# Jobs of the first layer moved in a hand-written timetable, and the second layer's first norm moved ahead of the layer boundary

## The reference, cut to what matters

```
mod = (silu(c) @ wmod).reshape(4, 6, 1, 128)            # sa, ca, ga, sb, cb, gb; |ga|, |gb| at least 0.25
# layer one
h = layernorm(x) * (1 + ca) + sa
x = x + ga * attn0(h)      # per token a 16-head recurrence: conv + silu on q, k, v, then
                           #   S = a*S - a*b*(S k) k^T + b*v k^T ;  o = q S      over 512 tokens; then @ Wo
h = layernorm(x) * (1 + cb) + sb
x = x + gb * ffn0(h)       # softmax routing, top 2 of 8 experts of 256 hidden columns
# layer two
h = layernorm(x) * (1 + ca) + sa
x = x + ga * attn1(h)      # differential causal attention, 16 heads, two softmaxes a head
h = layernorm(x) * (1 + cb) + sb
x = x + gb * ffn1(h)       # top 2 of 16 experts, plus a shared expert
```

## Time and profile before

| what | us |
|---|---|
| timed runs, in order | 1352.18, 1363.12, 1362.86 |
| median | 1362.86 |
| profiled execution | 1351.91 |
| its span, first instruction to last | 1349.8 |
| TensorE busy | 974.7 (72%) |
| VectorE busy | 836.9 (62%) |
| ScalarE busy | 583.0 (43%) |
| GpSimd busy | 442.2 (33%) |
| mean granted TensorE clock | 0.847 |

### The profile page before, as it was taken

How to read it: one execution, slowest core, us unless ns; L and a number is a source line. 1 busy time by engine, 2 the same in 40 slices (tenths; PEclk the granted TensorE clock), 3 DMA queues, 4 the chain that set the end, 5 groups by cost and what they waited for, 6 DMA issues and landing times.

```text
span 1349.8 us, 17349 instructions
## 1 busy us (share of the span) xinstructions
PE 974.7 (72%) x5737; PEld 579.8 (43%) x5737; DVE 836.9 (62%) x1960; ACT 583.0 (43%) x1409; POOL 442.2 (33%) x636
## 2 busy tenths in 40 slices
PE   5461465984986996787778788887777786865682
PEld 3231132453453553333335433454555553544482
DVE  1388879769988331766676666665656585624453
ACT  3344252462442343255454545334555543563262
POOL 0201341723733123022442244324312247323323
PEclk9785595996987997699788978669999987998797
DMA  8300000000000001000000000021244113341372
GB/s 233 94 0 0 1 0 1 1 3 33 1 1 1 1 0 40 0 1 1 1 1 1 1 1 1 1 72 59 83 126 115 61 49 119 94 117 53 116 224 83
DMA packets 54840, 60.39 MB, mean 45 GB/s; under 512 B 6224, under 2 KB 41184, under 8 KB 54752
## 3 DMA queue, kind: packets, MB, share of 16 engines
q1 hardware_dynamic: 52704, 55.10, 13.4%
q0 software_dynamic: 2048, 4.20, 1.0%
HBM read 46.05 MB, written 13.24 MB: 44 GB/s over the span
## 4 chain that ended last, share of the span: by engine, by line
PE 47%; DVE 20%; ACT 12%; issue 11%; POOL 7%; DMA 2%; SPq 0%; another core or an unknown queue 0%; ACTq 0%; DVEq 0%; POOLq 0%
PE banks L753 7%; PE banks L810 5%; PE banks L896 4%; PE banks L800 4%; PE banks L596 3%; POOL oms L1872 3%; DVE MX L1389 3%; PE banks L763 3%; PE banks L766 2%; PE banks L648 2%; PE banks L828 2%; PE banks L870 2%; ACT PT L1691 2%; PE banks L835 2%; ACT yh L1626 2%
## 5 line engine op out<-in xcount | busy, mean ns | idle before, releaser
L1389 DVE TENSOR_REDUCE MX<-banks 128x4 f32<-128x512 f32 (+2 forms) x192 | 199.2, 1043 | 89.9 <-PE banks L870 81.9
L1849 POOL TENSOR_SCALAR_AFFINE_SELECT PT<-PT 128x256 f32<-128x256 f32 x256 | 106.2, 428 | 412.2 <-ACT PT L1691 412.1
L1691 ACT ACTIVATE PT<-banks 128x768 f32<-128x768 f32 (+1 forms) x192 | 167.9, 878 | 108.4 <-PE banks L828 105.4
L753 PE MATMUL banks<-xgT,wg 128*128 128x128 f32 x616 | 89.2, 291 | 42.1 <-ACT ysb L1652 37.6
L835 PE MATMUL banks<-KS,QS 32*128 32x512 f32 (+3 forms) x512 | 97.7, 426 | 21.6 <-DVE MX L1389 17.3
L896 PE MATMUL banks<-PT,VA 128*17 128x512 f32 (+3 forms) x1024 | 98.5, 483 | 16.6 <-DVE on L1412 10.6
L800 PE MATMUL banks<-w,hid 128*128 128x128 f32 x512 | 77.1, 298 | 45.6 <-DVE hid L1334 43.4
L828 PE MATMUL banks<-QS,KS 32*128 32x128 f32 (+3 forms) x512 | 94.1, 411 | 13.9 <-ACT PT L1691 9.0
L800 PEld LDWEIGHTS banks<-w,hid 128*128 128x128 f32 x512 | 69.7, 206 | 78.9 <-DVE hid L1334 60.5
L753 PEld LDWEIGHTS banks<-xgT,wg 128*128 128x128 f32 x616 | 77.9, 199 | 55.1 <-issue 51.8
L1338 DVE SCALAR_TENSOR_TENSOR sil<-sil,yh 128x256 f32<-128x256 f32 x109 | 47.7, 438 | 61.2 <-ACT sil L1632 60.9
(11 more groups left out here) (266 smaller groups left out, 2098.1 us busy)
## 6 DMA issues: line engine op xcount, KB each, us to landing
wg<-in_ffn_dram SPq DMA_DIRECT2D x77, 386.0 KB
xg<-xs SPq DMA_DIRECT2D x17, 256.0 KB
yb<-ysb SPq DMA_DIRECT2D x17, 256.0 KB, 3.7
w<-in_ffn_w_dram SPq DMA_DIRECT2D x12, 256.0 KB
xs<-zt SPq DMA_DIRECT2D x2, 1472.0 KB, 14.2
xs<-zt SPq DMA_DIRECT2D x1, 1984.0 KB, 13.0
x<-in_L_attn_x_dram SPq DMA_DIRECT2D x4, 256.0 KB, 5.7
out_dram<-x SPq DMA_DIRECT2D x16, 64.0 KB
```

The lines of the kernel that those rows point to most:

```text
L753: mm = e.matmul(ps[:, at:at + cols], w, h, start=True, stop=True)
L1389: v_mx.at(e.tensor_reduce(MX[n % 2][:, u:u + nm, qb % 2, 2 * pair:2 * pair + 2, 24].rearrange("p s i -> p i s"), p4, AX.X, ALU.max, negate ...
L1691: a_p.at(e.activation(PT[q % 3][:, 2 * pair:2 * pair + 2, :], where["score", q, pair][:, :, 0:n], ACT.Exp, scale=ISQ8))
L1849: ins = e.affine_select(out=pt, in_=pt, compare_op=ALU.is_ge, fill=0.0, base=0, pattern=[[0, 2], [1, 128]], channel_multiplier=-1)
```

## The change

Only the tables change, and with them the order of jobs in layer one; one wait (`g_fin`) is split by tile. No operation is added or taken away.

- Post-scan jobs of groups 0 to 2: most stand 1 to 6 units of the table earlier, those of group 3 up to 3, in the part from `o_turn` to `route`.
- Experts: group 0 starts at 55 instead of 62 behind its scan with the same step of 4.6; group 1 at 55 with 3.7 instead of 4.6; group 2 at 55 with 3.1 instead of 4.0; group 3 at 39 instead of 42 with 2.7.
- Layer two's first `stat` and `norm` (batch 0) get the names `stat_x` and `norm_x` and stand at the end of layer one's table on VectorE and GpSimd: the statistics behind the last unit, the power between GpSimd's second and third `moe_x`. TensorE and ScalarE keep their part (`turn_x`) at the head of layer two.
- `stat` of layer two's batch m waits for 13 + m of the `moe_x` tiles instead of all 16.

```diff
@@ front_table
         if part == 0:
-            table += [(t - 14, ("stat", 0, 4 + b, (1, b))), (t - 9, ("norm", 0, 4 + b, (1, b)))]
+            if b:
+                table.append((t - 14, ("stat", 0, 4 + b, (1, b))))
+            table.append((t - 9, ("norm" if b else "turn_x", 0, 4 + b, (1, b))))
@@ LATE0
-    POOL=dict(stat=1.0, down=2.5, moe_x=1.0))
+    POOL=dict(stat=1.0, stat_x=2.0, down=2.5, moe_x=1.0))
@@ post_table
-        gq, state, pw, dk, ol, sums, out, step = 0, (1, 15), 5, 20, 21, (6, 20, 31), 34, 2.4
+        gq, state, pw, dk, ol, sums, out, step = 0, (1, 14), 5, 18, 19, (6, 19, 29), 31, 2.2
...
-    table += [(sums[2], ("o_sum", g, 2)), (out, ("o_tok", g)), (out + 3, ("o_turn", g)), (out + 5, ("o_out", g))]
-    table += [(out + 7 + i, ("o_x", g, i)) for i in range(3)]
-    table += [(out + 11, ("stat", 1, g, (0, g))), (out + 14, ("norm", 1, g, (0, g)))]
-    table += [(out + 19 + 1.6 * i, ("route", g, i)) for i in range(6)]
+    table += [(sums[2], ("o_sum", g, 2)), (out, ("o_tok", g)), (out + 2.5, ("o_turn", g)), (out + 4, ("o_out", g))]
+    table += [(out + 6 + i, ("o_x", g, i)) for i in range(3)]
+    table += [(out + 10.5, ("stat", 1, g, (0, g))), (out + 13, ("norm", 1, g, (0, g)))]
+    table += [(out + 17 + 1.4 * i, ("route", g, i)) for i in range(6)]
@@ table_layer0
-        table += post_table(g, SCAN[g + 1]) + moe0_table(g, SCAN[g + 1] + (62 if g < 3 else 42), (4.6, 4.6, 4.0, 2.7)[g])
-    return table
+        table += post_table(g, SCAN[g + 1]) + moe0_table(g, SCAN[g + 1] + (55 if g < 3 else 39), (4.6, 3.7, 3.1, 2.7)[g])
+    end = max(t for t, job in table if job[0] == "moe_x") - 3
+    return table + [(end + 0.5, ("stat_x", 0, 4, (1, 0))), (end + 2, ("norm_x", 0, 4, (1, 0)))]
@@ VectorE, stat
                 elif k == 0:
-                    v.wait_ge(g_fin, 16)
+                    v.wait_ge(g_fin, 13 + m)
```

More of the change, by code:

```diff
@@ L86 @@
 LATE = dict(
-    PE=dict(norm=2.0, top_t=4.0, o_back=2.5),
+    PE=dict(norm=2.0, turn_x=2.0, top_t=4.0, o_back=2.5),
     DVE=dict(top=2.0, top_t=6.0, qk_in=2.0, up=4.0, down=1.0, route=2.0, place=0.0, w_o=2.0, rms=2.5),
-    ACT=dict(score=1.0, qk_in=1.0, v_in=1.0, norm=3.0, turn=1.0, up=1.5, rms_t=1.0, route=4.0, gate_t=1.0),
+    ACT=dict(score=1.0, qk_in=1.0, v_in=1.0, norm=3.0, turn_x=3.0, turn=1.0, up=1.5, rms_t=1.0, route=4.0, gate_t=1.0),
     POOL=dict(score=2.5, o_norm=1.5, w_o=3.0, stat=1.5, moe_x=1.0),
@@ L932, in w_o @@
                 busy[i] = [(v_xq, b + 1)]
-            jobs = dict(table=table, mod=mod, gate=gate, norm=norm, route=route, qkv=qkv, ab=ab_in, conv=conv,
+            jobs = dict(turn_x=norm, table=table, mod=mod, gate=gate, norm=norm, route=route, qkv=qkv, ab=ab_in, conv=conv,
                         turned=turned, k_t=k_t, vq_t=vq_t, ab_t=ab_t, o_sum=o_sum, o_tok=o_tok, o_turn=o_turn, o_out=o_out,
@@ L1441, in w_o @@
                                         ga[1][0][:, b:b + 1, :].broadcast_to([128, 4, 128]), ALU.mult))
-            jobs = dict(blend=blend_, mod=mod, gate=gate, gate_s=gate_s, lam=lam_, stat=stat, norm=norm, route=route,
+            jobs = dict(stat_x=stat, norm_x=norm, blend=blend_, mod=mod, gate=gate, gate_s=gate_s, lam=lam_, stat=stat, norm=norm, route=route,
                         ab=ab_in, share=share, invlen=invlen, ab_t=ab_t, dk=dk, gm=gm_, kb=kb, vb=vb, ga=ga_,
@@ L1702, in rms_t @@
                 a_to.at(e.activation(oTs[k][:, :], where["rms_t", b, k][:, :], ACT.Copy))
-            jobs = dict(table=table, mod=mod, lam=lam_, tok=tok_, diag=diag, norm=norm, route=route, qkv=qkv, decay=decay, conv=conv,
+            jobs = dict(turn_x=norm, table=table, mod=mod, lam=lam_, tok=tok_, diag=diag, norm=norm, route=route, qkv=qkv, decay=decay, conv=conv,
                         turned=turned, k_t=k_t, vq_t=vq_t, ab_t=ab_t, scan=scan, o_sum=o_sum, o_tok=o_tok, o_turn=o_turn,
@@ L1885, in _ @@
             g_zero.at(e.memset(Sb[0][:, 0, :, :], 0.0))
-            jobs = dict(stat=stat, length=length, pairs=pairs, ktd=ktd, o_gq=o_gq, o_state=o_state,
+            jobs = dict(stat_x=stat, stat=stat, length=length, pairs=pairs, ktd=ktd, o_gq=o_gq, o_state=o_state,
                         o_pw=o_pw, o_dk=o_dk, o_ol=o_ol, down=down, spread=spread, collect=collect,
```

## The result

The changed kernel is slower: a median of 1381.76 us (1379.55 to 1384.6), against 1362.99 us (1352.18 to 1366.88) for the one before beside it, a ratio of 1.0148 (95% interval 1.0095 to 1.0201; a ratio here is that of the comparison, not the quotient of the two medians, which is 1.0138). I had forecast 1358 and a range up to 1369. Its profiled execution took 1383.42 us, of a span of 1381.4. Lines of the changed file are three higher than before: the scan's first operation is L1266, the reduction at a step's end L1278, an output sum L651, `up` L766 and L769, `down` L803, `hid` L1337.

The account below looks back on a forecast made before the run. No engine alone was taken to bound the kernel, so stages were priced singly: scans +1.0, end of layer one -4.5, first norm -1.2, together -4.7 us. From the median of 1362.86 that gives 1358 us, range 1340 to 1369.

Parts of the forecast that it names:

- the end of scan 3, E: End of scan 3, at 418.8 us before; forecast to move by +1.0 us and to lie within 416 to 423.
- anything over 425: Sign of being wrong: scan 3's end over 425, with gaps before GpSimd's adds or VectorE's `o_x` in scan 3.
- Three more `hid`, +2.0: VectorE up to scan 3's end: three more expert multiplications of 0.68 us each, +2.0 us.
- Relief of scan 2, -2.5: Scan 2: earlier `hid` lets TensorE resume early and bring work forward, -2.5 us, bounds -4.3 and -1.7.
- Scan 3, +1.5, bounds 0 and +4.2: Scan 3: GpSimd's add of unit 11 waits and delays group 2's outputs, which pass it to the scan, +1.5 us.
- Rival C: Scan 3: GpSimd's in-order adds hold up group 2's outputs, 12.5 us instead of 1.5; +6.3 in all, 1369 us; chance 0.13.
- The end of layer one, -4.5 (bounds -2 and -11.3): Behind scan 3: TensorE's lighter list brings group 3's third up from 60.2 to 55.7 us behind the scan's end.
- The first norm, -1.2: Start of layer two: statistics and power run beside GpSimd's adds, transposes start 1.2 us earlier, bounds 0 and -3.0.
- Layer two, 0: Layer two behind its first transposes: as long as before; later loads and memsets at its head cost nothing, at most 1.5 us.
- D: Rival: the scans lose 1 to 3 us and absorb the 2 that the end gains; 0 +- 2, 1363 us; chance 0.15.
- Rival E: Behind scan 3: TensorE's clock stays low at up 11 and first sum, +3.7; -1.0 in all, 1362 us; chance 0.08.
- The two levels of 11 us: Three timed runs before read as two levels 11 us apart; a median on the lower level would be 1347 us.

Follow-up runs that it names:

- run 6: Kernel before with only the second output sum of groups 0 to 2 moved from unit 20 to 19; ratio 1.0076, 1367.96 us.
- run 3: Kernel before with only the experts' starts and steps changed, as in the full change; ratio 1.0038.
- run 5: Kernel before with only the experts changed, but group 1's kept at its old start and step (62, 4.6); ratio 0.9999.
- run 9: Kernel before with the moved norm, group 0's experts from 55 and group 3's from 41, the rest as before; ratio 1.0001.
- run 1: Changed kernel with the second output sum of groups 0 to 2 put back from unit 19 to 20; ratio 1.0081, 1372.88 us.
- run 2: Kernel before with only the table of post-scan jobs changed, experts and norm as before; ratio 1.0098.
- run 7: Changed kernel with ScalarE's expert copies later in its own list (up 1.0 to 2.5, down 1.5 to 2.5); 1377.17 us, ratio 1.0154.
- run 11: As run 9, but group 2's experts from 62 at 3.1 apart and group 3's from 39; ratio 1.0003.
- run 4: Kernel before with only the first norm of layer two moved ahead of the layer's end; ratio 1.0007.
- run 10: As run 9, with ScalarE's expert copies later in its own list (up 1.0 to 2.5, down 1.5 to 2.5); ratio 0.999.
- run 12: As run 9, with the second output sum of groups 0 to 2 moved from unit 20 to 24; ratio 0.9964.

## Why the prediction was wrong

**The step that failed** is the sum for the end of scan 3, E: "+2.0 - 2.5 + 1.5 = +1.0", measured +28.4 (E at 447.2, where I had called anything over 425 a sign of being wrong). Scan 1 has no term of its own in it beyond two `hid`, and the term of scan 3 has the wrong cause. The prediction says that what counts is which job stands ahead of which, and then counts TensorE's work in windows and GpSimd's adds. It never lists, for each moved job, the neighbour that it passes on its own engine, nor what is queued on ScalarE behind the copy of that neighbour. Both were to be had from the table: 163.0 against 163.8, and the convolution's copy with the scan copy behind it, being the chain that waits. What the runs showed in the place of +1.0: the swapped sum alone costs 5.3 us of scan 1 and 3.4 of scan 3 (run 6), and the packed experts alone 12.5 of scan 3 (run 3), most of it waiting of scan steps for ScalarE's copies (in run 3's scan 3 the idle time ahead of the step's last operation is 15.8 us instead of 6.3).

**Three more `hid`, +2.0.** Right: x37 and 25.2 us before, x40 and 27.2 after. But VectorE's busy time over the scans is the same, 215.1, since small operations between the steps got shorter by as much, so it isn't work that made E later.

**Relief of scan 2, -2.5.** Right where it is alone (-2.8 in run 5, -3.7 in run 9). In the changed kernel scan 2 took 2.4 more: scan 1's loss pushes the scan steps, and the two waits of 11.1 and 11.4 us fell only to 9.0 and 8.1, where I had said 6 or less. The first down isn't earlier at all (228.88, before 228.62), although its `hid` is seven units ahead, since the list runs 9 us late by the end of scan 1:

```profile
228.88 2.08 PE L803 MATMUL banks<-w,hid 128*128 128x128 f32 x8 [9.04 <-DVE hid L1337]
...
332.33 2.07 PE L766 MATMUL banks<-hTr,w 128*128 128x512 f32 x2 [8.08 <-DVE hid L1337]
```

**Scan 3, +1.5, bounds 0 and +4.2.** Measured +16.6. Of the experts' 12.5, group 1's packing has 5.6 and group 2's 6.9; the sum's place has 5.4 (run 1). These overlap in part with each other and with the rest of the post-scan jobs, as 12.5 + 5.5 (run 2) is 18.0 and not 16.6. Rival C named this scan, the right direction, and the wrong engine: its 1369 is nearer to the result than my 1358 by luck. GpSimd's waits in this stretch after are these:

```profile
358.07 1.27 POOL L1815 TENSOR_TENSOR acc<-acc,yt 128x512 f32<-128x512 f32 x1 [5.95 <-ACT yt L1671]
359.30 1.14 POOL L1760 TENSOR_TENSOR GQ<-Q,GM 128x512 f32<-128x512 f32 x1
360.52 4.49 POOL L1773 TENSOR_TENSOR QX<-GQ,Sb 128x512 f32<-128x512 f32 x4
...
368.35 1.27 POOL L1815 TENSOR_TENSOR acc<-acc,yt 128x512 f32<-128x512 f32 x1 [0.61 <-ACT yt L1671]
```

An add waits 5.95 us and the first `o_state` starts 4.9 us behind the scan's start instead of 0.4 ahead of it; the add of unit 11, for which I had worked out 0 to 2, waited 1.97. So C's mechanism exists, as a delay of the sums. But the idle time of the scan ends with ScalarE's copy in 58.8 of 61.0 us, and two of the causes were undone without a change at GpSimd (runs 1 and 7). What an add's wait alone costs was not measured.

**The end of layer one, -4.5 (bounds -2 and -11.3).** Measured -2.8 to the third up and -1.1 from there to the last `hid`, -3.9 in sum. The path was as drawn up to `o_x`: the chain passes `o_pw`, hid 9, up 11 and the three sums, and the first `o_x` is at 486.20, E+39.0, where I had E+40.4. Behind it I was 3.1 us short, and most of that is TensorE's clock, for which this stage had no term. With group 2 packed from 55, TensorE has nothing left while the norm is made:

```profile
492.96 0.77 PE L558 MATMUL banks<-ident,xn 128*128 128x128 f32 x2 [4.26 <-DVE xn L1027]
...
496.48 1.88 PE L571 MATMUL banks<-gw,hTr 128*128 128x8 f32 x8 [1.66 <-ACT hTr L1499]
498.21 2.05 PE L766 MATMUL banks<-hTr,w 128*128 128x512 f32 x2
500.06 1.92 PE L769 MATMUL banks<-hTr,w 128*128 128x512 f32 x2
501.77 1.91 PE L766 MATMUL banks<-hTr,w 128*128 128x512 f32 x2
...
504.57 1.02 PE L766 MATMUL banks<-hTr,w 128*128 128x512 f32 x2
```

After the idle 4.26 us the granted clock is 0.50 from 494 to 502. The gate's product takes 1.88 us for eight, against 0.95 at the same place in run 9, and ends at E+51.2, where I had it: the lead of 1.4 us is used up, half of it already at the norm's end (E+47.1, forecast E+47.8). The first `hid` ends at E+55.6, also as drawn up (the terms give E+55.9, I wrote 55.7). But the third up starts only at E+57.4, 1.7 us behind the forecast, because TensorE's first two ups, which take 1.02 a row at the upper level, stand ahead of it with 2.05, 1.92 and 1.91. In run 11, where group 2 is packed but starts at 62, the clock here is 1.00 and the third up follows the first `hid` at E+56.2.

The pace from the third up on had no term. From there to the last `hid` it took 36.6 us in the changed kernel and in runs 1, 3, 5 and 7, all with group 2 packed from 55 and group 3 from 39, 38.4 in run 11 and 37.7 in the others; why is open.

**The first norm, -1.2.** Measured -1.1, alone (run 4) and in the full change. The power stands among GpSimd's adds as forecast (549.67 to 550.69, the last add behind it at 552.14), and the transposes wait for the memset:

```profile
552.14 0.45 POOL L1828 TENSOR_TENSOR x<-x,acc 128x128 f32<-128x128 f32 x1
...
552.96 0.48 DVE L1455 MEMSET banks<- 128x512 f32 x1 [0.29 <-DVEq L1453]
...
553.54 1.08 PE L558 MATMUL banks<-ident,xn 128*128 128x128 f32 x4 [8.92 <-DVE banks L1455]
```

The last add ends at 552.59 and the transposes start 0.95 later; I had 0.8.

**Layer two, 0.** It took 825.0 against 816.8, which is 8.2 of the 31.6 us between the two spans. In all fourteen profiles it lies between 811.3 and 826.8, and its code is the same in run 9 (815.2), run 10 (826.8), run 11 (824.6) and run 12 (814.8), all with the moved norm. Without the moved norm it was 822 to 823 in runs 3, 5 and 6. So the 8.2, and the 7.1 of run 4, can't be put down to the change; that the moved norm adds a few us on average isn't excluded. The measured medians differ by 18.8 us, less than layer one's 23.1. What sets layer two's length from run to run stays open.

**D and E.** D had the scans absorb what the end gives up; the end gave 5.0 and the scans took 28.2. Rival E had the lower clock at up 11 and the first sum behind the scan. There it isn't: the first sum is on the chain with 3.58 us, the upper level. The lower level came later, at the gate's product and the first ups of group 3, and cost about 2.4 of the 3.1 us above (1.7 at the ups and 0.7 at the gate's product), an estimate from these rows.

**The two levels of 11 us.** I read three timed runs as two levels, and put the lower end of the range on one of them. The 35 timed runs of the kernel before that stand beside run 9 spread from 1349.76 to 1374.27 with no gap over 3.8 us. So there is a spread and no lower level to fall on.

## What to carry to other kernels

Where every engine runs its own fixed list, price a moved job by its neighbours: name the job that it passes on its engine, ask whether the moved one is ready there, and follow the passed one's consumer to what is queued behind it on the next engine; here a move of one sum by one unit, past a convolution or an `up`, cost 0.8% (run 6). Busy time in windows doesn't show this, the idle time ahead of the critical chain's own operation does, with what ended it. And side work whose copies stand among those of the chain may be packed only as far as its own ring (product, copy, freed bank, next product) lets enough steps of the chain pass: packing group 2 (with group 3 two units earlier) gave 3.7 us behind the scan and cost 5.6 in it.

## What the runs showed of the hardware

TensorE's clock made a wait dearer than its length. The same eight products of an output sum took 3.65 us at the upper level (2.4 GHz) before, and 5.34 after a wait of 2.09 us. In the changed kernel the granted clock was still 1.00 when the sum began at 175.14; it fell behind that, to 0.50 (1.2 GHz) from 177 to 179, and was back at 1.00 from 180 on. Ahead of the sum TensorE had made four transposes (172.39, 0.66 us) and then waited. In the kernel before, it was busy without such a wait, and the clock was 1.00 throughout this place. So waiting and lower clock together are 3.8 us here. Run 6 repeats it with the same 5.34 us, and a granted clock of 0.50 from 178 to 180.

VectorE's product of 128 columns with two inputs takes 0.29 us alone; beside GpSimd's product of 1024 columns (176.03, 1.98 us) it took 1.69 us and ended at 178.16, just behind it. Over the three scans the two such groups took 86.5 us after and 83.1 before. I had put 1.3 us on it. The Trainium skill, SBUF — State Buffer, section "SBUF: two separate sides", says that the shared pair is locked for a whole instruction and the loser waits; the trace agrees, with 1.69 against 0.29. But VectorE's busy time as a whole did not grow: three `hid` (2.0 us) and these two groups (3.4) are made up by small operations between the steps that took less. So this isn't where the 28 us went.
